# A fused recurrence, attention output and feed-forward kernel: unread products, one weight sizing, two rounding steps, an addend and a down product taken out or moved

## What is computed

```python
def step(S, inp):                       # one chunk of 16 tokens
    qi, ki, vi, ei = inp
    kh = jnp.einsum('bchd,bhde->bche', ki, S)
    target = vi - ki
    mu = jnp.mean(kh, -1, keepdims=True)
    rstd = jax.lax.rsqrt(jnp.var(kh, -1, keepdims=True) + EPS)
    kh_hat = (kh - mu) * rstd
    g = w * kh_hat + b - target
    gw = g * w
    v_new = (gw - jnp.mean(gw, -1, keepdims=True) - kh_hat * jnp.mean(gw * kh_hat, -1, keepdims=True)) * rstd
    A = jnp.einsum('bchd,bshd->bhcs', qi, ki)
    A = jnp.where(tri, A, 0.0) * jnp.transpose(ei, (0, 2, 1))[:, :, None, :]
    qh = jnp.einsum('bchd,bhde->bche', qi, S) - jnp.einsum('bhcs,bshe->bche', A, v_new)
    o = qi + _ln(qh, w, b)
    S = S - jnp.einsum('bchd,bche->bhde', ki * ei[..., None], v_new)
    return (S, o)
...
x = x + _layernorm(_L0_attn_ref(_layernorm(x, axis=-1), ...), axis=-1)
x = x + _layernorm(_L0_ffn_ref(_layernorm(x, axis=-1), ...), axis=-1)
```

## Time and profile before

| | |
|---|---|
| time, median of 3 runs | 848.6 us (847.11 to 849.54) |
| profiled execution: its time | 848.27 us |
| profiled execution: its span | 846.5 us |
| mean granted TensorE clock | 0.979 of full speed |
| busy: PE | 771.3 us (91%) |
| busy: DVE | 668.0 us (79%) |
| busy: ACT | 512.5 us (61%) |
| busy: POOL | 480.2 us (57%) |

### The profile page before, as it was taken

The page is one execution under the profiler, slowest core; times in us unless marked ns, Lnnn a source line. Parts: engine busy times, 40 slices in busy tenths (PEclk is TensorE's granted clock), DMA queues, the critical chain, the costliest instruction groups (busy, mean ns, idle before and its releaser), DMA issues.

```text
span 846.5 us, 24475 instructions
## 1 busy us (share of the span) xinstructions
PE 771.3 (91%) x9068; PEld 589.4 (70%) x9068; DVE 668.0 (79%) x2689; ACT 512.5 (61%) x1356; POOL 480.2 (57%) x853
## 2 busy tenths in 40 slices
PE   7877778687889999999999999999999999979996
PEld 4656555565777686777777686777877777767795
DVE  2788997887897888878887888788887888769644
ACT  1797878687786466656556474666565564732332
POOL 5466767565756657565565647565655657437300
PEclk9899997999999999999999999999999999999999
DMA  8012120201210010000100010000100010000000
GB/s 285 28 51 64 39 76 27 75 27 43 72 39 27 2 39 14 27 3 2 51 2 26 2 53 2 27 2 2 52 2 27 2 51 2 2 1 27 26 26 26
DMA packets 16727, 28.58 MB, mean 34 GB/s; under 512 B 3520, under 2 KB 3520, under 8 KB 16608
## 3 DMA queue, kind: packets, MB, share of 16 engines
q1 hardware_dynamic: 16608, 27.02, 9.9%
HBM read 22.82 MB, written 4.19 MB: 32 GB/s over the span
## 4 chain that ended last, share of the span: by engine, by line
PE 63%; DVE 18%; POOL 8%; ACT 4%; issue 4%; SPq 1%; DMA 1%; ACTq 0%; DVEq 0%; POOLq 0%
PE bank L683 19%; PE bank L463 10%; PE bank L718 10%; PE bank L659 5%; PE bank L630 4%; POOL rho L1332 3%; PE bank L477 3%; PE bank L603 3%; PE bank L616 2%; DVE work L1666 2%; PE bank L497 2%; PE bank L638 2%; DVE work L1670 1%; DVE SQ L1682 1%; PE bank L513 1%
## 5 line engine op out<-in xcount | busy, mean ns | idle before, releaser
L1332 POOL TENSOR_TENSOR rho<-sy,cst 128x2 f32<-128x2 f32 x128 | 89.6, 700 | 200.1 <-DVE sy L1639 200.1
L630 PEld LDWEIGHTS bank<-VX,BDkR 128*64 128x64 f32 x1024 | 43.8, 138 | 61.5 <-issue 26.5
L630 PE MATMUL bank<-VX,BDkR 128*64 128x64 f32 x1024 | 56.7, 232 | 30.7 <-DVE VX L1675 29.8
L1038 ACT ACTIVATE qhR<-bank 128x64 f32<-128x64 f32 x128 | 28.5, 223 | 92.0 <-PE bank L638 91.6
L997 ACT ACTIVATE BDkR<-kR,cst 128x128 f32<-128x128 f32 x256 | 81.6, 400 | 0.0
L983 ACT ACTIVATE BDk<-bank 32x256 f32<-32x256 f32 x124 | 46.6, 376 | 57.3 <-DVE kR L1581 48.6
L1682 DVE TENSOR_TENSOR SQ<-SQ,bank 128x128 f32<-128x128 f32 x128 | 36.6, 286 | 53.9 <-PE bank L630 52.2
L1661 DVE SCALAR_TENSOR_TENSOR work<-work,rho,rR 128x32 f32<-128x32 f32 x256 | 53.2, 249 | 28.2 <-POOL rho L1332 26.8
L603 PEld LDWEIGHTS bank<-SQ,BDk 128*64 128x64 f32 x1024 | 45.9, 139 | 41.5 <-issue 39.1
L603 PE MATMUL bank<-SQ,BDk 128*64 128x48 f32 x1024 | 55.1, 227 | 16.4 <-DVE SQ L1682 15.1
L683 PE MATMUL bank<-xh,GW 128*128 128x256 f32 x384 | 65.1, 292 | 3.4 <-DVE xl L1732 3.0
(11 more groups left out here) (194 smaller groups left out, 2179.1 us busy)
## 6 DMA issues: line engine op xcount, KB each, us to landing
xt<-in_x SPq DMA_DIRECT2D x16, 256.0 KB, 2.7
x<-in_x SPq DMA_DIRECT2D x16, 256.0 KB, 2.8
out<-x SPq DMA_DIRECT2D x16, 256.0 KB, 2.0
yb<-in_gate_w SPq DMA_DIRECT2D x12, 256.0 KB, 2.6
yb<-in_up_w SPq DMA_DIRECT2D x12, 256.0 KB, 2.6
yb<-in_down_w SPq DMA_DIRECT2D x12, 256.0 KB, 2.6
Wk<-in_wk SPq DMA_DIRECT2D x1, 1024.0 KB, 7.9
Wv<-in_wv SPq DMA_DIRECT2D x1, 1024.0 KB, 9.8
```

The costliest lines, as they stand in the source:

```text
L630: ins = mm(dS[p, e], bdkr[:, gh, j % 4, p], VX[:, e], start=True, stop=True, skip_group_check=True)
L1332: tt(dst, src, cst[:, C_NH:C_NH + n], ALU.pow).then_inc(*one)
```

## The change

It has seven parts. (1) The unread products go from chunk 4 of tiles 0, 1 and 2 and from chunk 7 of tile 0; those of (0, 6) and of the start stay. (2) The addend for tile 1's queries goes from POOL at (0, 4) to VectorE at (1, 0), in a new function second_qb, which stands between VX and the update of S. (3) quantize of the unit of (1, 2) goes to the end of (1, 3). (4) The units of (3, 6) and (4, 6) are sized by ScalarE, at (3, 5) and (4, 5), straight behind the unit of chunk 5. (5) norm_rs of tiles 1 and 3 goes behind the other POOL steps of chunk 6; in tile 1 nothing stands between the two places. (6) In tile 15 the down product of round 5 goes from chunk 3 to chunk 2, its ffn_fh and ffn_fl from chunk 2 to the end of chunk 1. (7) Conditions elsewhere follow these. No arithmetic of the result is left out.

```diff
--- before.py
+++ after.py
@@ -351,7 +351,7 @@
         def by_scalar(u):
 
             t, j = next((t, j) for t in range(NT) for j in range(NC) if u in unit_before(t, j))
-            return j in (1, 2, 3, 4, 5) or (j == 6 and early(t + 1))
+            return 1 <= j <= 6
 
         def sized(u):
             n = sum(by_scalar(m) == by_scalar(u) for m in range(u + 1))
@@ -799,9 +799,10 @@
                             prep_k(t + 1)
                     if j == 3 and early(t + 1):
                         prep_v_early(t + 1, (0, 1, 2))
-                    if j == 3 and t == NT - 1:
+                    if j == 2 and t == NT - 1:
                         ffn_down(*ffn[0], 0)
                         ffn_down(*ffn[0], 1)
+                    if j == 3 and t == NT - 1:
                         ffn_g(*ffn[1])
                     elif j == 3 and 1 in ffn:
                         ffn_g(*ffn[1])
@@ -818,7 +819,6 @@
                     if j == 4 and early(t + 1):
                         prep_v_early(t + 1, (3,))
                         pe.wait_ge(*(prep_v.at("kR", t) if t else prep_v.at("rR", 0)))
-                        idle(3, cst)
                     elif j == 4 and prep:
                         prep_vv(t + 1, False)
                     if j == 5 and t < NT - 1:
@@ -852,7 +852,6 @@
                         post_wo(t - 1)
                     if j == 7 and t == 0:
                         prep_gate(1)
-                        idle(2, cst)
                     if scan and rounding(t):
 
                         read_queries(t, j, s)
@@ -1191,11 +1190,13 @@
                         fn(thT[:, :], U4[:, :], ACT.Tanh, scale=0.5).then_inc(*prep_a.one("th"))
                     elif j == 0 and early(t + 1):
                         prep_xnT(t + 1)
-                    if j == 2 and 0 in ffn:
+                    if j == 2 and 0 in ffn and t < NT - 1:
                         ffn_fh(*ffn[0])
                     from_exponent(t, j)
-                    if not early(t + 1) and j not in (1, 4):
+                    if not early(t + 1) and j in (2, 3, 5):
                         from_weight(t, j)
+                    if not early(t + 1) and j == 5:
+                        from_weight(t, 6)
 
                     if j == 0:
                         if early(t):
@@ -1263,6 +1264,8 @@
                     if scan:
                         take_qh(t, j, s)
                     if t == NT - 1:
+                        if j == 1:
+                            ffn_fh(*ffn[0])
                         if j == 4:
                             ffn_fh(*ffn[1])
                         if j == 5:
@@ -1500,11 +1503,11 @@
                             if scan:
                                 after_rows(NC * t + 2)
                             post_nw(t - 1)
-                    if j == (6 if rounding(t) else 2) and norm and s:
+                    if j == 2 and norm and s and not rounding(t):
                         norm_rs(t + 2)
                     if j == 3 and prep:
                         prep_rk(t + 1)
-                    if j == 4 and prep:
+                    if j == 4 and prep and t > 0:
                         after_rows(NC * t + 4)
                         prep_qb(t + 1, o)
                     if j == 5 and post:
@@ -1518,7 +1521,7 @@
                             ffn_fl(*ffn[1])
                         if prep and not early(t + 1):
                             prep_b1(t + 1)
-                        if norm and not s:
+                        if norm and (not s or rounding(t)):
                             norm_rs(t + 2)
                     if j == 7 and fin:
                         fin_ry(h - 2, 0)
@@ -1680,6 +1683,14 @@
                 c = NC * n + j
                 dve.wait_ge(scan_t.sem, scan_t.at("upd", c))
                 tt(S, S, dS.rearrange("p (g e) -> p g e", e=DH), ALU.add).then_inc(*scan_v.one("S"))
+
+            def second_qb():
+
+                dve.wait_ge(*prep_v.at("qR", 1))
+                dve.wait_ge(*prep_g.at("qb", 0))
+                m = qR[1][:, :].rearrange("p (gh j e) -> p gh j e", gh=2, e=DH)
+                tt(m, m, bR[:, :].rearrange("p (gh e) -> p gh e", gh=2).unsqueeze(2).broadcast_to([P, 2, NC, DH]),
+                   ALU.add).then_inc(*prep_g.one("qb"))
 
             def post_qss(n):
                 dve.wait_ge(post_a.sem, post_a.at("qsq", n))
@@ -1895,6 +1906,8 @@
 
                     if j == 0 and post:
                         post_qss(t - 1)
+                    if j == 0 and t == 1:
+                        second_qb()
                     if j == 0 and t == 0:
                         prep_qR(0, 0)
                     if j == 1 and scan:
@@ -1943,6 +1956,8 @@
                             tail_x1(t - 2)
                         if norm and s:
                             x_stats(t + 2)
+                        if t == NT - 1:
+                            ffn_fl(*ffn[0])
                     if j == 2:
                         if s and is_pair(h - 1):
                             pair_xl(h - 1)
@@ -1982,10 +1997,15 @@
                         if fin:
                             fin_out(h - 2, 0)
 
+                    if (t, j) == (1, 3):
+
+                        for u in unit_before(1, 2):
+                            quantize(u)
                     for u in unit_before(t, j):
                         if not pool_free(t, j):
                             shift(u)
-                        quantize(u)
+                        if (t, j) != (1, 2):
+                            quantize(u)
                     for u in unit_at(t, j):
                         exponent(u)
```

## The result

The change made the kernel slower: 852.04 us (median of 11 runs, 849.97 to 853.44) against 847.6 us (11 runs of the kernel before on the same chip, 845.83 to 849.54). The ratio is 1.0041, 95% interval [1.0026, 1.0056], so about 3.5 us slower (4.4 between the medians), where 4.3 faster was forecast. The profiled execution took 850.41 us, span 848.6, mean granted clock 0.970 (before 0.979).

What follows compares the result with a forecast made beforehand. It took a serial chain of waits over PE, VectorE and POOL as the bound, with PE bounding the drain. Terms summed to -4.3 us, from the 848.6 us median to 844.3 us; range 841.3 to 847.6 us.

Steps and rivals of the forecast that it cites:

- (H): Tiles 0 to 2: removed products leave PE idle, one more half-clock stretch, +0.9 us, bounds 0 and +3.8.
- rival 1: All four places of removed products fall to half clock: +3.8 instead of +0.9 us, 847.2 us; chance 0.09.
- (D): Unread products removed: write at (1, 4) starts earlier, -0.3 us, bounds 0 and -0.7; nothing at the other places.
- (E): At (3, 5) and (3, 6), ScalarE sizing and later norm_rs shorten VectorE's wait for b1: -1.3 us, bounds -2.1 and +1.6.
- (F): Same ScalarE sizing for (4, 6), norm_rs already behind: -0.3 us, bounds -0.9 and +1.6.
- (G): Tile 15, down product moved from chunk 3 to 2: VectorE's 2.48 us idle goes, -2.6 us, bounds -0.9 and -2.8.
- rival 5: Drain does not start earlier, last tile's gain swallowed or hidden: 846.9 us; chance 0.04.
- Rival 2: Last tile gains only its full-clock part, -0.9 instead of -2.6 us: 846.0 us; chance 0.14.
- (A): Addend leaves POOL at (0, 4), so VectorE's last rounding step takes 0.69, not 1.71 us: -1.0 us, bounds 0 and -1.0.
- (B): Addend on VectorE at (1, 0), beside POOL's shift, delays the update of S: +0.4 us, bounds 0 and +1.2.
- (C): One weight's rounding moves from (1, 2) to (1, 3): 0.75 gained, 0.69 returned; -0.1 us, bounds -0.7 and +0.3.
- rival 4: Half clock throughout tiles 0 to 2: measurably slower from eight new stretches, 852.0 us with nine; chance 0.06.

Runs made afterwards that it cites:

- idle_only: Kernel before with the unread products of chunk 4 of tiles 0 to 2 and chunk 7 of tile 0 removed, nothing else; ratio 1.0049, 851.86 us.
- idle4_only: Kernel before without the unread products of chunk 4 of tiles 0 to 2, keeping those of chunk 7 of tile 0; ratio 1.0032, 850.78 us.
- idle7_only: Kernel before without the unread products of chunk 7 of tile 0, keeping the others; ratio 1.0027, 850.35 us.
- all_but_idle: Kernel after with the removed unread products put back at all four places; against the kernel before, ratio 1.0013, 848.79 us; repeated, 1.0001, 848.11 us.
- size_only: Kernel before with only the units of (3, 6) and (4, 6) sized by ScalarE at chunk 5 and norm_rs moved behind; ratio 0.9993, 847.89 us.
- fill_36: tail_size plus two pairs of unread products ahead of the transposes in (3, 6); against the kernel before, ratio 0.9938, 843.94 us.
- tail_size: Kernel before with the last tile's down product moved and the ScalarE sizing of (3, 6) and (4, 6), norm_rs behind; ratio 0.9975, 845.32 us.
- quant_only: Kernel before with only the rounding of one weight unit moved from (1, 2) to (1, 3); ratio 1.0002, 848.07 us.
- qb_quant: Kernel before with only tile 1's query addend and one weight unit's rounding moved; ratio 1.0009, 848.39 us.
- all_filled: Whole change with its unread products put back and those of warm and fill_36 added; against the kernel before, ratio 0.9936, 843.39 us.
- qb_only: Kernel before with only tile 1's query addend moved from POOL at (0, 4) to VectorE at (1, 0); ratio 0.9995, 848.02 us.
- warm: tail_size plus unread products ahead of the write in (0, 0), (1, 3), (2, 2) and (2, 3); against the kernel before, ratio 0.9977, 845.54 us.

## Why the prediction was wrong

The forecast was -4.3 us, the measurement +3.5. The steps, in the order of the prediction:

- **(H), the clock, is the step that failed.** It took one more stretch of half clock at 0.95 us. Over all executions the removal alone (idle_only) brings 21.6 us of half clock, some six stretches of 3.4 us (five in the profiled execution), and by time it costs +4.2 us [2.4, 5.8] alone, about 3 inside the change (1.0041 against 1.0013 and 1.0001). The price was about right: 4.2 us for 21.6 is 0.7 per 3.4 us, idle4_only and idle7_only make 0.8 and 0.9; in the kernel after's profile the grown chunks make 5.9 for four more stretches, 1.5 each. The count was wrong, and the reason that rival 1 gives for it: "these lie beside three of the four places, so little is new". The rows had PE busy for 1.87 of 4.80 us ahead of the fall in tile 15, and step (D) wrote that the products' absence "opens nothing there but PE's idle time". That idle time was what cost.
- **(H) also counted for the removal alone.** With the products in place the other parts bring 16.7 and 12.7 us of half clock (all_but_idle and its repetition), four to five stretches that stood in no term.
- **(E) and (F)** had the right size at full clock, and left the clock out. Forecast -1.6; size_only measures -0.6 [-2.1, +0.9], from which neither the forecast nor no gain can be told. BDk in (3, 5) is 1.6 us late, as worked out, and is recovered: (3, 6) falls from 9.56 to 7.8 us where the clock holds. In fill_36 (3, 5) to (3, 7) are 1.4 us shorter than before and (4, 5) to (4, 7) 0.4 (forecast 1.3 and 0.3). Left out was that PE, waiting 2.1 to 2.2 us for bt, may fall as well; then (3, 6) is 9.0 to 9.2, and the six chunks together are 0.5 us shorter (the kernel after) or 0.8 longer (tail_size).
- **(G)** held: tile 15 is 2.9 us shorter in the kernel after's profile (forecast 2.6), by time -1.9 [-3.8, -0.1], and the drain starts earlier and lasts the same, 74.0 and 74.1 us, which disposes of rival 5. Rival 2's point, that the half clock part may stay, holds for some executions. Where no half clock stands near 750 us with the old order either (quant_only, 38.25 us), the gain is 1.3.
- **(A)** held in its chunk, 1.0 us, as did the mechanism. **(B)**, forecast +0.4, costs 0.7 at full clock: (1, 0) lasts 5.28 us in qb_quant and all_filled, 4.56 in quant_only and tail_size. By time qb_only, which holds both, shows nothing (-0.4 us [-2.2, +1.3]).
- **(C)** held, -0.2 us: from the statistic of (1, 2) to rho of (1, 3) it is 5.5 us in place of 6.3, the 0.8 that the step worked out, and the rounding comes back in (1, 3). The statistic of (1, 3) itself starts 1.9 us earlier, so VectorE waits 0.67 for rho [the row at 88.16]. The half clock that the move puts on (1, 5) was in no term.
- **(D)** gave nothing, forecast 0.3. (1, 4) lasts 5.77 us in the kernel after and 5.76 in all_but_idle, which has the products; and 5.60 in idle_only and in tail_size alike. The 0.2 us against before's 5.96 have another cause.
- Without (D) and (H) the terms made -4.9, and all_but_idle measured +1.1 and +0.1. At full clock the parts are worth -1.0, +0.7, -0.2, -1.8 and -1.3, so -3.6; the half clock of these two kernels is, by estimate, +3.9 and +3.0. That makes +0.3 and -0.6, within both intervals. The same sum for the kernel after (55.0 us of half clock, 31 to 36 in the kernels before) makes +0.8 to +2.0, for a measured +3.5 [2.2, 4.7]; what it lacks is not found.
- Small slips of the sums: the terms of the range's lower end make 841.5, not 841.3, and rival 4's eight stretches make 851.0, just under its own line of 851.1. The sum starts from 848.6, the median of 3 runs; that of the 11 is 847.6. None of it bears on the outcome.

Of the rivals, number 4 had the sign and the time (852.0) and 6% of the chance; its place was tiles 0 to 2, as found, its count of nine stretches was too high by the executions' clocks (19 to 24 us of half clock, six to seven stretches), since other terms gave less than the 5.2 us it set against them. Rival 1, all four places at half clock, was the mechanism in the narrower sense, priced at 3.8 us; the products' removal measures 4.2. What the Trainium skill says on "TensorE: Matmul & The Clock Gate", section "Why this matters for your kernels", that TensorE should not be left idle between bursts in mid-kernel, is borne out by the traces of the kernel after and of idle_only: 1.30, 1.05, 0.49, 1.12 and 0.90 us busy of 3.4 us, each with half clock behind it. The prediction cited it and gave it 0.09.

The reason was read from the wrong side. It asked what the removed products delayed, and found little; what they kept up was not asked, though the earlier trace rows showed that the clock falls in this kernel.

## What to carry to other kernels

In a chain bound by latency, work on TensorE whose result nobody reads can be load-bearing: before it is taken out, list for each place how long PE is idle around it and what runs on PE next, and price every such place as a stretch at half clock. The same holds for a step moved onto an engine that PE waits for: a new wait of 2 us costs itself and the clock behind it, and two pairs of unread products in it gave back 3 us. Move one part at a time and time it over several executions, since parts of 1 to 3 us gave back what others gained. Where every execution has its mean clock on record, read it for all of them: it told idle7_only's loss and warm's missing gain, where the one profile of each said the contrary.
